# Fetching one tile of every second block row by row from two other queues, in a graph layer bound by gathers

## The reference

```
h    = relu(layernorm(x))                        # 12500 x 128
m    = relu(concat(h[src], edge_attr) @ msg_w1 + msg_b1) @ msg_w2 + msg_b2     # 400000 x 128
agg  = segment_sum(m, dst)                       # 12500 x 128
out  = x + relu(concat(h, agg) @ upd_w1 + upd_b1) @ upd_w2 + upd_b2
```

## Time and profile before

| | |
|---|---|
| median of 3 runs | 3937.84 us (3936.56 to 3939.78) |
| the profiled execution | 3936.85 us, its span 3935.0 us |
| busy: POOL / TensorE / VectorE / ScalarE | 75% / 62% / 37% / 14% of the span |
| mean granted TensorE clock | 0.73 of full speed |
| mean traffic | 87 GB/s |

### The profile page before, as it was taken

The page is one execution under the profiler, slowest core; times in us unless marked ns, Lnnn a source line. Parts: engine busy times, 40 slices in busy tenths (PEclk is TensorE's granted clock), DMA queues, the critical chain, the costliest instruction groups (busy, mean ns, idle before and its releaser), DMA issues.

```text
span 3935.0 us, 32488 instructions
## 1 busy us (share of the span) xinstructions
PE 2438.7 (62%) x10672; PEld 2096.1 (53%) x10672; DVE 1449.3 (37%) x1593; ACT 537.6 (14%) x629; POOL 2952.3 (75%) x3133
## 2 busy tenths in 40 slices
PE   6596656565666566666656665665666665666565
PEld 4585555554555555555545555555555555555555
DVE  6673333333333333333333333333333333344433
ACT  6321111011111101111110111111111111111111
POOL 7777777777777777777777777777777777777776
PEclk9797777767776777777777766777776777777776
DMA  8232222223222222222222222222222222343322
GB/s 229 86 104 84 78 81 81 77 77 85 77 77 80 81 77 77 85 76 77 79 84 77 77 85 77 77 77 85 77 77 85 77 77 77 100 114 108 111 82 71
DMA packets 154626, 340.77 MB, mean 87 GB/s; under 512 B 73896, under 2 KB 74920, under 8 KB 154188
## 3 DMA queue, kind: packets, MB, share of 16 engines
q0 software_dynamic: 100000, 205.00, 19.9%
q1 hardware_dynamic: 46165, 121.97, 9.8%
q10 hardware_dynamic: 8406, 13.14, 1.0%
HBM read 327.06 MB, written 12.81 MB: 86 GB/s over the span
## 4 chain that ended last, share of the span: by engine, by line
POOL 52%; issue 21%; PE 14%; DMA 6%; DVE 4%; ACT 1%; ACTq 0%; POOLq 0%; SPq 0%; DVEq 0%
POOL rows L392 26%; POOL x_all L392 26%; PE pre L475 7%; PE seg L521 4%; DMA x_all<-table,index 2%; DMA rows<-table,index 2%; DVE rows L965 1%; DVE x_all L965 1%; DMA x_all<-in_x 1%; PE spare L569 1%; ACT rows L740 1%; DVE space L1005 1%; PE pre L496 1%; PE pre L505 0%; PE spare L536 0%
## 5 line engine op out<-in xcount | busy, mean ns | idle before, releaser
L475 PE MATMUL pre<-w_attr_sb,attrs 128*128 128x256 f32 x3126 | 1347.8, 604 | 1370.0 <-DVE rows L965 684.7
L392 POOL DMA_INDIRECT x_all<-table,index x1536 | 1449.1, 943 | 468.1 <-issue 457.4
L392 POOL DMA_INDIRECT rows<-table,index x1517 | 1434.0, 945 | 472.1 <-issue 451.4
L475 PEld LDWEIGHTS pre<-w_attr_sb,attrs 128*128 128x128 f32 x3126 | 908.8, 306 | 1607.3 <-DVE rows L965 702.3
L965 DVE TENSOR_TENSOR x_all<-pre,x_all 128x1024 f32<-128x1024 f32 x192 | 234.9, 1224 | 1134.0 <-DMA x_all<-table,index 1127.0
L965 DVE TENSOR_TENSOR rows<-pre,rows 128x1024 f32<-128x1024 f32 (+1 forms) x190 | 232.1, 1222 | 1100.7 <-DMA rows<-table,index 1095.9
L521 PEld LDWEIGHTS seg<-space,rows 128*128 128x128 f32 x3178 | 472.3, 227 | 27.8 <-ACT rows L728 5.2
L521 PEld LDWEIGHTS seg<-space,x_all 128*128 128x128 f32 x3072 | 462.6, 229 | 23.0
L521 PE MATMUL seg<-space,rows 128*128 128x80 f32 x3178 | 450.2, 304 | 5.0 <-ACT rows L728 4.8
L1019 DVE TENSOR_REDUCE h_space<-space 128x240 f32<-128x1920 f32 x130 | 440.8, 3390 | 0.0
L521 PE MATMUL seg<-space,x_all 128*128 128x80 f32 x3072 | 438.5, 306 | 0.0
(11 more groups left out here) (80 smaller groups left out, 529.3 us busy)
## 6 DMA issues: line engine op xcount, KB each, us to landing
attrs<-in_attr SPq DMA_DIRECT2D x130, 768.0 KB
x_all<-table,index POOLq DMA_INDIRECT x1536, 2.5
rows<-table,index POOLq DMA_INDIRECT x1517, 2.5
table<-rows SPq DMA_DIRECT2D x25, 224.0 KB
h_space<-in_x ACTq DMA_DIRECT2D x13, 224.0 KB
out<-h_space ACTq DMA_DIRECT2D x13, 224.0 KB
x_all<-in_x ACTq DMA_DIRECT2D x12, 224.0 KB
out<-x_all ACTq DMA_DIRECT2D x12, 224.0 KB
```

The source lines that it names most:

```text
L392: pool.indirect_dma_start(slot_rows(j)[:, t, :], None, source, bass.IndirectOffsetOnAxis(index[0:EDGES, j, t:t + 1], 0))\
L475: return pe.matmul(columns(j, q, PAIR)[:, two * 2 * D:(two + 1) * 2 * D], attrs[:, j % 2, start:start + EDGES], w_attr_sb[:, :], start=Tru ...
```

## The change

The eighth tile of the last pair of a block is no longer gathered by POOL in every second block, the odd ones from block 9 to block 129 (61 of 122 blocks by the condition in the code, 60 in the change's title). Its 128 rows are fetched by 128 DMAs of one row (512 bytes) each: for the slots 3 and 7 from the SP queue (30 tiles), for the slots 1 and 5 from ACT's queue (31 tiles). The indices of these edges are loaded once into a new SBUF tile `index_rows` (16 partitions). The rows of a tile are spread over the four blocks that lie five to two blocks ahead of it: 32 rows in a block on either queue. SP issues its 32 after the attributes of the block; ACT issues 8 after the relu of pair 0, 8 after that of pair 1 and 16 after that of pair 2, and in the last 18 blocks that is ahead of the chain that finishes groups. Eight indices at a time are loaded into registers; then each row is one DMA whose source address comes from a register. VectorE waits, besides for the gathers, for a new semaphore `rows_landed`.

```diff
+BY_SP = (3, 7)
+BY_ACT = (1, 5)
+BATCH = 8
+BATCHES = P // BATCH
...
+        def single(i, j):
+            b = block_of(i, j)
+            return j in BY_SP + BY_ACT and (not isinstance(i, int) or i >= 1) and (not isinstance(b, int) or b < LAST)
...
+        def gathers(i, j, q):
+            return tiles_of(block_of(i, j), q) - (1 if q == PAIRS - 1 and single(i, j) else 0)
...
+        def fetch_rows(engine, i, j, slots, part, parts):
+            positions = 4 if len(slots) == 2 else 2
+            for s in slots:
+                for k in range(positions):
+                    if (s - 2 - k) % SLOTS != j:
+                        continue
+                    round_of = i + 1 if s - 2 - k < 0 else i
+                    if not single(round_of, s):
+                        continue
+                    target = block_of(round_of, s)
+                    column = (round_of * len(BY_SP + BY_ACT) + (sorted(BY_SP + BY_ACT).index(s) - len(BY_SP + BY_ACT))) * BATCH
+                    each = BATCHES // positions
+                    first = (positions - 1 - k) * each
+                    for n in range(first + part * each // parts, first + (part + 1) * each // parts):
+                        if n == first:
+                            engine.wait_ge(hidden_summed, (target - SLOTS) * PAIRS + PAIRS)
+                        site = next(fetches)
+                        registers = [engine.alloc_register(f"row{m}_of_fetch{site}") for m in range(BATCH)]
+                        engine.load(registers, index_rows[n:n + 1, bass.ds(column, BATCH)])
+                        for m in range(BATCH):
+                            p = n * BATCH + m
+                            row = bass.RuntimeValue.of_register_unchecked(registers[m], min_val=0, max_val=N - 1)
+                            engine.dma_start(slot_rows(s)[p:p + 1, TILES_B - 1, :], table[bass.ds(row, 1), :]).then_inc(rows_landed[s], 16)
...
+            sp.dma_start(index_rows[:, :], src_rows).then_inc(index_rows_loaded, 16)
...
                 load_attr(i, j)
+                if BY_SP:
+                    fetch_rows(sp, i, j, BY_SP, 0, 1)
...
-                    gather(table, j, range(q * PAIR, q * PAIR + tiles_of(b, q)))
+                    gather(table, j, range(q * PAIR, q * PAIR + gathers(i, j, q)))
...
                     relu_hidden(i, j, q)
+                    if BY_ACT:
+                        fetch_rows(act, i, j, BY_ACT, q, PAIRS)
...
-                    dve.wait_ge(gathered[j][q], i * (16 * PAIR) + 16 * tiles)
+                    dve.wait_ge(gathered[j][q], landings(i, j, q))
+                    if q == PAIRS - 1 and single(i, j):
+                        dve.wait_ge(rows_landed[j], i * (16 * P))
```

More of the change, by code:

```diff
@@ L36, in after, with gnn_layer @@
     return step + (CREDIT + 1 - back)
-def gnn_layer(nc, x, src, src_last, dst_rows, dst_cols, attr, attr_last, w_src, w_attr, b_msg1, w_msg2_t, b_msg2, w_node, w_agg, b_upd1,
+def gnn_layer(nc, x, src, src_last, src_rows, dst_rows, dst_cols, attr, attr_last, w_src, w_attr, b_msg1, w_msg2_t, b_msg2, w_node, w_agg, b_upd1,
               w_upd2, b_upd2, out):
@@ L167, in gnn_layer @@
         rel = sb("rel", [P, PAIR])
+        index_rows = sb("index_rows", [BATCHES, src_rows.shape[1]], I32)
         pre = ps("pre", [P, 2, 1024])
@@ L233, in gnn_layer @@
         index_next_loaded = sem("index_next_loaded")
+        index_rows_loaded = sem("index_rows_loaded")
+        rows_landed = [sem(f"rows_landed{j}") for j in range(SLOTS)]
         index_early_loaded = sem("index_early_loaded")
@@ L285, in ahead, with landings @@
             return (i, j + blocks) if j + blocks < SLOTS else (i + 1, j + blocks - SLOTS)
+        def single(i, j):
+            b = block_of(i, j)
+            return j in BY_SP + BY_ACT and (not isinstance(i, int) or i >= 1) and (not isinstance(b, int) or b < LAST)
+        def landings(i, j, q):
+            full = 16 * PAIR
+            if q < PAIRS - 1 or j not in BY_SP + BY_ACT or (isinstance(i, int) and i == 0):
+                return i * full + 16 * tiles_of(block_of(i, j), q)
+            return full + i * (full - 16)
+        def gathers(i, j, q):
+            return tiles_of(block_of(i, j), q) - (1 if q == PAIRS - 1 and single(i, j) else 0)
+        fetches = itertools.count()
+        def fetch_rows(engine, i, j, slots, part, parts):
[21 more added lines that the diff above has]
+                            engine.dma_start(slot_rows(s)[p:p + 1, TILES_B - 1, :], table[bass.ds(row, 1), :]).then_inc(rows_landed[s], 16)
         def behind(i, j, blocks):
@@ L368, in load_block @@
                 load_attr(i, j)
+                if BY_SP:
+                    fetch_rows(sp, i, j, BY_SP, 0, 1)
+            sp.wait_ge(index_rows_loaded, 16)
+            for k in range(UNROLL):
+                sp.wait_ge(table_stored[k], 16 * len(CUT) * GBODIES)
             sp.wait_ge(update_ready, after(GROUPS - 1))
@@ L755, in relu_block @@
                     relu_hidden(i, j, q)
+                    if BY_ACT:
+                        fetch_rows(act, i, j, BY_ACT, q, PAIRS)
+            if BY_ACT:
+                act.wait_ge(index_rows_loaded, 16)
+                for k in range(UNROLL):
+                    act.wait_ge(table_stored[k], 16 * len(CUT) * GBODIES)
             for j in range(EARLY, SLOTS):
@@ L1230 @@
     width = attr.shape[2]
+    fetched = [b for b in range(SLOTS, blocks) if b % SLOTS in BY_SP + BY_ACT]
+    edges = np.concatenate([np.arange(EDGES) + (b * TILES_B + TILES_B - 1) * EDGES for b in fetched])
     arrays = {
         "x": x,
+        "src_rows": src[edges].reshape(len(fetched), BATCHES, BATCH).transpose(1, 0, 2).reshape(BATCHES, -1),
         "src": src[:body].reshape(blocks, TILES_B, EDGES).transpose(0, 2, 1), "src_last": src[body:].reshape(-1, EDGES).T,
```

## The result

The kernel before took 3937.38 us in these runs (3936.56 to 3939.78, 4 runs), the changed kernel **3879.68 us** (3876.23 to 3880.77, 4 runs). The ratio is 0.9852 [0.984, 0.9864]: 1.5% faster, where 0.48% was forecast. 3919 us was 39 us too high.

What follows compares the result with a forecast made beforehand. POOL's gathers, 1.249 us each, were taken as the bound. 3936.85 - 76.2 (gathers) + 48.5 (end) + 8.4 (start) + 0.5 (index load) = 3918.1; with the median 0.99 higher, 3919 us, range 3864 to 3988.

Steps and rivals of the forecast that it cites:

- the gain: Blocks 9 to 129, odd: 61 gathers fewer on POOL at 1.249 us each, 76.2 us saved.
- The steady loop: Main loop: SP's 23.3 us and ACT's 22.4 + 0.3 us a block hide within POOL's 29.35, cost 0.
- the margin: At pair 0 of a block, ACT may be about 9 us late before POOL stops.
- the term c: Price of one row on SP or ACT: 0.70 us, 0.50 issue plus 0.20 load; bounds 0.59 and 0.79.
- The start: Blocks 4 to 15: ACT needs 22.7 us a block, so POOL waits 8.4 us once, at block 16.
- The end: Blocks 112 to 121: ACT's rows and the finish chain add, so POOL waits 48.5 us.
- the formula of the prediction: Last blocks: 32c + 11.9 us a block against POOL's 29.35; first lateness 16c + 1.7, nine further excesses, less 9 of margin.
- The chain of 11.6 us: Last blocks: finish chain of two groups, 4.2 us for the first and 7.3 from there to the next block's relu.
- the likeliest case: Whole kernel: part of the gain kept, c from 0.58 to 0.79, 3877 to 3978 us, chance 0.62.
- All of it is gained: Rival for the last blocks: ACT's rows fit beside the finish chain or c is under 0.57; 3862 to 3870 us, chance 0.10.
- ACT's queue becomes the bound: Rival for blocks 4 to 15 and 112 to 121: c above 0.75, kernel slower, 3985 us at 0.80; chance 0.24.
- One DMA engine gets all rows: Rival on row transfers: 26 of 29.35 us a block, hidden; at twice the packet cost over 5000 us in all; chance 0.04.

Runs made afterwards that it cites:

- rows_after_2: Changed kernel with ACT's 16 rows of pair 2 issued behind the finish chain in the last 18 blocks: 3862.53 us, 0.9807 of the kernel before.
- warm: Changed kernel plus unread TensorE products ahead of the finish chain (16 before a block's first group, 8 before the second): 3875.14 us, 0.9839 of the kernel before.
- sp_all: Changed kernel with all 64 rows a block on SP, none on ACT, on a slower chip: 6669.37 us against 4717.36 for the kernel before.

## Why the prediction was right in sign and wrong in size

**Right.** The bound (POOL's pace) and the gain: 76.2 us, of which `rows_after_2` realises 75.6. The steady loop hides the rows: no wait over 0.3 us. VectorE does not wait longer than before. ACT's rows and the chain add in the last blocks. And the margin: the relu of 3358.04 was due 10.0 us behind that of the pair before (3337.41), so it was 10.6 us late. POOL stopped for 1.75 us, so the margin is 8.9, with 9 forecast.

**The step that failed: the term c, "What a row costs on SP or ACT".** 0.70 was built from 0.50 for the issue and 0.20 for the load; measured were 0.38 and some 0.15, with ACT's own relus inside the 0.53. Both rows chosen were too dear. The stores of the earlier trace rows move 128 partitions, and their issue takes 0.32 us; a row's takes 0.22, which is shorter than any issue in the earlier trace rows. So an issue is not of one price, and the lower bound (0.44) came from DMAs that are dearer than a row. That their size is the reason is likely; no run varies the size alone. The load was extrapolated in a straight line from one and three registers, which gave 1.82 us for eight on VectorE; it is 0.73 on ACT and 0.70 on SP. The one-register row of 0.566 in the same group, the lower bound, would have given 1.20 and was too dear as well. The two rows of one register already differed by 0.25 us (0.317 and 0.566), so one of them could not carry the slope of a line.

The Trainium skill (Advanced Engine Details and Errata, Clock Domains) would have changed this by 0.01 us a row, and the sum by 7. The runs say nothing for or against its clocks: none has loads of the same number of registers on VectorE and on ACT or SP.

**What followed from it.** The start, 8.4 us, was nothing: ACT's block there is 17 us, not 22.7. The end, 48.5 us, was 15 to 16, by two edits that take it away. VectorE's longer waits for the chain came as forecast (by the name of `h_space`, 134.5 us against 66.0).

**A second term, of the other sign, was too small.** With c = 0.53 the formula of the prediction gives 32 x 0.53 + 11.9 = 28.9 us a block, less than POOL's 29.35, so only the first lateness would count: 16 x 0.53 + 1.7 - 9 = 1.2 us. That would have been 3863, and 16 us too low. The chain of 11.6 us was put together from a block in which TensorE had just run and nothing was late. Its two groups take 13.1 us behind the rows. With the measured 30.89 us a block the prediction's formula gives 10.6 - 8.9 + 9 x (30.89 - 29.35) = 15.6 us, which is what POOL lost. Rows and chain alone took 30.3 in the block shown, so the 30.89 hold some 0.6 of waits that the formula does not have. But for these the form of the sum was right, and two sizes in it were wrong in opposite directions. That 3880 lies just inside the range of the likeliest case (3877 to 3978) is luck: c was below its lower bound of 0.59. Some 7 to 9 us of POOL's loss go away when the clock is held at 1.00, as `warm` shows. The Trainium skill (TensorE: Matmul & The Clock Gate, "What's actually happening") has the clock fall back to its lower level when TensorE is idle; the trace agrees, 0.50 after 4.71 us without a product and 1.00 with the extra products ahead of the chain. The rest is likely the feedback: a stop of POOL makes the gathers behind it late, the next relus with them, and so the lateness doesn't shrink. That this is the remaining part is argued from the timelines and not tested by itself.

Two slips in the recorded sums change nothing: the dearer load is 0.23 us a row and not 0.24, and c = 0.80 gives 3985 in one place and 3988 in another.

**The rivals.** "All of it is gained" (0.10) is what `rows_after_2` is, with c under its 0.57; the changed kernel lies between it and my case. "ACT's queue becomes the bound" did not occur here with 32 rows; `sp_all` shows its form. "One DMA engine gets all rows": nothing waits for rows. Each row is two packets, one of 512 bytes and one of 4. By the trace's single packets the first takes some 0.03 us and the second 0.009, so 0.020 on average. The mean packet of 0.134 us, from which this rival was priced, was nearly seven times too dear. The queues' shares agree: q1 and q10 together have 267 us more (q1 6199 against 6170, q10 868 against 630) for 15,648 packets more, 0.017 us each, with the rounding of the shares worth half of that. Even on one engine the 64 rows of a block would be some 2.5 us of 29.35, an estimate from these packets. Since each row has only one packet of 512 bytes, it isn't split over engines. Whether all rows go over the same one the profile doesn't say.

## What to carry to other kernels

When an operation that the trace does not show is priced from its nearest rows, ask in which size they differ from it (partitions and registers here), and let the lower bound go below the nearest row. When a second queue takes work over, look for the chains on that queue that something waits for, and put the new work behind them: the same 16 rows behind the chain in place of ahead of it are worth 16 us. And a chain that is cut loose from its neighbours' work may find TensorE at its lower clock.

## What the hardware did that I had not expected

- A DMA of one row of 512 bytes, its address in a register, takes 0.22 us to issue, and they follow each other about 0.38 us apart on ACT and 0.41 on SP; a store over 128 partitions takes 0.32.
- A load of eight registers from SBUF takes 0.73 us on ACT and 0.70 on SP, of four 0.51 on ACT, of three 0.75 on VectorE.
- The 7,808 rows, with two packets each, added some 0.3 ms to 62 ms of the 16 DMA engines, about 0.04 us a row.
- Eight products took 2.04 us in place of 1.11 after 4.71 us without work.
- With the longer loops on SP and ACT, the queue of instructions carried 284 packets in place of 28.
- The same program takes 3937 us on some chips and 4715 to 4756 on others, and two edits that are worth 1.8 and 1.9% on the former cost 10 and 11% on the latter.
